# A decoder block on one core: experts' rows are added onto the residual rows in DRAM instead of being stored twice and summed at the end

## The reference, cut to what matters

```python
x = _layernorm(x + linear_attention(x))                       # 16 x 256 tokens of 256 features
x = _layernorm(x + cross_attention(x, ctx))
h = x + attention_over_the_batch_axis(layernorm1(x))          # hidden_after_attn, the residual rows
y = layernorm2(h)                                             # 4096 tokens
gate = softmax(y @ router.T); top_probs, top_idx = top_k(gate, 2)
expert_out[e] = gelu(y @ w1[e]) @ w2[e]                       # 8 experts, 256 -> 512 -> 256
x = _layernorm(h + sum_e weights[e] * expert_out[e])          # two experts for every token
```

## Time and profile before

| | |
|---|---|
| time, median of 3 runs | 800.7 us (794.5 to 801.46) |
| the profiled execution | 791.32 us, of which the span is 789.6 us |
| first scatter of the experts' loop | 477.25 us from the span's start |
| last scatter of the loop | 727.62 us |
| ending | from 730.07 us to the span's end |
| mean granted TensorE clock | 0.896 of full speed |

### The profile page before, as it was taken

One profiled execution on the slowest core, in us unless ns is written; L12 is line 12 of the kernel. 1 busy time (PEld: TensorE's weight loads), 2 busy tenths in 40 slices (PEclk: granted clock), 3 DMA queues, 4 the chain that ended last, 5 costly groups with the idle time before them and its releaser, 6 DMA issues.

```text
span 789.6 us, 19124 instructions
## 1 busy us (share of the span) xinstructions
PE 628.5 (80%) x5128; PEld 536.9 (68%) x5137; DVE 539.7 (68%) x1853; ACT 391.5 (50%) x923; POOL 321.0 (41%) x439
## 2 busy tenths in 40 slices
PE   4889999999961989999965139999999999997000
PEld 3678998898840667777755128888888888886000
DVE  1337878887855466888884836777777777775772
ACT  1335666656625556666534415555555555553233
POOL 0025777677643002566676722222222222222431
PEclk9989999999985899999976559999999999999555
DMA  6062444344311000111111422222222222221873
GB/s 196 0 177 71 143 133 113 106 138 123 97 28 27 1 2 2 42 56 57 56 56 68 154 91 70 72 80 68 79 68 79 69 80 68 80 68 47 279 245 114
DMA packets 48605, 69.19 MB, mean 88 GB/s; under 512 B 10577, under 2 KB 35281, under 8 KB 48561
## 3 DMA queue, kind: packets, MB, share of 16 engines
q1 hardware_dynamic: 40144, 46.30, 20.1%
q0 software_dynamic: 6480, 17.87, 6.1%
q10 hardware_dynamic: 1936, 4.46, 2.0%
HBM read 40.21 MB, written 24.19 MB: 82 GB/s over the span
## 4 chain that ended last, share of the span: by engine, by line
PE 42%; DVE 11%; DMA 5%; issue 3%; ACT 3%; POOL 3%; SPq 2%; DVEq 0%; POOLq 0%; ACTq 0%
PE half_bank L145 9%; PE half_bank L147 9%; PE half_bank L146 9%; PE half_bank L1856 5%; DMA out_dram<-all_w 3%; PE half_bank L1373 2%; PE half_bank L1837 2%; PE half_bank L1449 2%; POOL dispatched L949 2%; PE half_bank L1361 1%; DVE region_k_diag L1216 1%; ACT all_w L1615 1%; PE half_bank L1460 1%; DVE region_v_turned L1229 1%; DVE region_prob L1244 1%
## 5 line engine op out<-in xcount | busy, mean ns | idle before, releaser
L1675 POOL DMA_INDIRECT results<-all_w_qkv,ex_home x71 | 68.3, 961 | 200.6 <-DVE all_w_qkv L1800 170.5
L1707 ACT ACTIVATE region_hid_hi<-half_bank 128x256 fp32r<-128x256 f32 x142 | 46.9, 381 | 79.3 <-PE half_bank L1856 79.2
L949 POOL DMA_INDIRECT dispatched<-all_xh,all_slot_u x64 | 68.6, 1072 | 34.0 <-DVE all_slot_u L1318 17.4
L145 PE MATMUL half_bank<-region_w_hi,region_hid_hi 128*128 x284 | 81.2, 286 | 1.1 <-DVE region_hid_lo L1792 1.1
L146 PE MATMUL half_bank<-all_w,region_hid_hi 128*128 x284 | 79.7, 281 | 0.0
L147 PE MATMUL half_bank<-region_w_hi,region_hid_lo 128*128 x284 | 79.4, 280 | 0.0
L1694 ACT ACTIVATE all_xh<-half_bank,all_ln_b,all_ln_w 128x128 f32<-128x128 f32 x142 | 57.8, 467 | 21.0 <-PE half_bank L1837 21.0
L1800 DVE TENSOR_SCALAR all_w_qkv<-half_bank,ex_gate 128x256 f32<-128x256 f32 x71 | 34.3, 483 | 48.7 <-PE half_bank L147 48.7
L145 PE MATMUL half_bank<-region_w_hi,region_x_hi 128*128 x142 | 62.9, 443 | 0.7 <-DVE region_x_lo L1785 0.7
L1701 ACT ACTIVATE all_w_proj<-half_bank 128x512 f32<-128x512 f32 x71 | 42.5, 599 | 40.0 <-PE half_bank L147 40.0
L145 PEld LDWEIGHTS half_bank<-region_w_hi,region_hid_hi 128*128 128x128 f32 x284 | 53.3, 188 | 11.3 <-issue 7.8
(11 more groups left out here) (241 smaller groups left out, 1809.3 us busy)
## 6 DMA issues: line engine op xcount, KB each, us to landing
all_xh<-dispatched SPq DMA_DIRECT2D x71, 130.5 KB, 2.1
all_w<-in_moe_w_dram SPq DMA_DIRECT2D x32, 256.0 KB, 3.1
all_w<-results SPq DMA_DIRECT2D x12, 512.0 KB, 6.7
all_resid<-at_x SPq DMA_DIRECT2D x32, 128.5 KB
shared_x_t<-in_x_t_dram SPq DMA_DIRECT2D x16, 256.0 KB, 4.2
at_x_tok<-in_x_dram SPq DMA_DIRECT2D x16, 256.0 KB, 4.3
out_dram<-all_w ACTq DMA_DIRECT2D x6, 512.0 KB
dispatched<-all_tail SPq DMA_DIRECT2D x8, 261.0 KB, 3.3
```

Source lines behind the costliest of these rows:

```text
L145: nc.tensor.matmul(out, a_hi, b_hi, start=(start and i == 0), stop=False)
L949: nc.gpsimd.indirect_dma_start(out=dram["dispatched"], out_offset=bass.IndirectOffsetOnAxis(ap=keep["slot_u"][g % SENDS][:, u, k:k + 1], a ...
L1675: nc.gpsimd.indirect_dma_start(out=dram["results"], out_offset=bass.IndirectOffsetOnAxis(ap=home[par][:, 0:1], axis=0), in_=ym[par], in_of ...
L1707: nc.scalar.activation(hid_hi[par][:, cs, :], p_t[half], ACT.Copy).then_inc(s["hid_high"], 1)
```

## The change

The buffer `results` has one row for every token and the spare rows (4352 rows in place of 8448). SP stores the residual rows there (`store_base`), one group at a time: seven groups while the attention over the batch axis still runs, ahead of SP's other work there, and the last behind the first two loads of the experts' loop. GpSimd waits for all eight before its first scatter. Each scatter carries an addition, so a token's row collects the residual and both experts' rows. The place of a row is the token's number alone. The ending loads one sum per token. DVE's two additions go, and the freed space gives both the loads and the stores eight buffers.

```diff
-    DEPTH = 4
+    DEPTH = 8
...
-    y_rows = w1[:, :, :].rearrange("p k f -> p (k f)").rearrange("p (i k t d) -> p i k t d", i=DEPTH, k=2, d=D)
-    out_rows = w2[:, 0:2 * WIDEST, :].rearrange("p (i t) d -> p i t d", i=2)
+    y_rows = w1[:, :, :].rearrange("p k f -> p (k f)").rearrange("p (i t d) -> p i t d", i=DEPTH, d=D)
+    out_rows = w2[:, :, :].rearrange("p (i t) d -> p i t d", i=DEPTH)
...
         for j, (first, wide) in enumerate(TURNS):
             i = j % DEPTH
             wait(sp, out_ready, j - DEPTH + 1)
-            for k in range(2):
-                sp.dma_start(y_rows[:, i, k, 0:wide, :], dram["results_of"][k][:, first:first + wide, :])\
-                  .then_inc(y_in[i], 16)
+            sp.dma_start(y_rows[:, i, 0:wide, :], dram["sums"][:, first:first + wide, :]).then_inc(y_in[i], 16)
...
-        dve.wait_ge(keep["keep_done"], GROUPS * 2)
         for j, (first, wide) in enumerate(TURNS):
             i, par = j % DEPTH, j % 2
-            rows, more = y_rows[:, i, 0, 0:wide, :], y_rows[:, i, 1, 0:wide, :]
-            dve.wait_ge(y_in[i], (j // DEPTH + 1) * 32)
-            steps.chain(V.tensor_tensor(rows, rows, more, ALU.add))
-            steps.chain(V.tensor_tensor(rows, rows, keep["resid"][:, first:first + wide, 0:D], ALU.add))
+            dve.wait_ge(y_in[i], (j // DEPTH + 1) * 16)
             wait(dve, shift_ready, j - 1)
-            layer_norm_stats(steps, nc, rows, en_stats[par], en_mv[par], var_ready)
+            layer_norm_stats(steps, nc, y_rows[:, i, 0:wide, :], en_stats[par], en_mv[par], var_ready)
...
-            wait(act, out_stored[par], j // 2 * 16)
+            wait(act, out_stored[i], j // DEPTH * 16)
...
+        def store_base(g):
+            sp.wait_ge(keep["keep_done"], 2 * g + 2)
+            sp.dma_start(dram["sums"][:, g * NI:(g + 1) * NI, :], keep["resid"][:, g * NI:(g + 1) * NI, 0:D])\
+              .then_inc(base_out, 16)
+
+        for g in range(GROUPS - 1):
+            store_base(g)
         sp.wait_ge(s["tails_ready"], 1)
...
         load(0, 0)
         load(1, 1)
+        store_base(GROUPS - 1)
         with sp.Fori(0, (MOE_TILES - 3) // 2) as j:
...
             nc.gpsimd.indirect_dma_start(
                 out=dram["results"], out_offset=bass.IndirectOffsetOnAxis(ap=home[par][:, 0:1], axis=0),
-                in_=ym[par], in_offset=None).then_inc(ym_out[par], 16)
+                in_=ym[par], in_offset=None, compute_op=ALU.add).then_inc(ym_out[par], 16)
+        pool.wait_ge(base_out, GROUPS * 16)
         send(0, 0)
...
-            steps.chain(V.scalar_tensor_tensor(home_f[par][:, :], hit[:, 1:2], float(TOKENS), token[par][:, 0:1],
-                                               ALU.mult, ALU.add))
+            steps.chain(V.tensor_copy(home_f[par][:, :], token[par][:, 0:1]))
...
-        dram["results"] = scratch("results", [2 * TOKENS + 2 * P, D])
+        dram["results"] = scratch("results", [TOKENS + 2 * P, D])
```

More of the change, by code:

```diff
@@ L1022, in gpsimd_program @@
         nc.gpsimd.memset(tail[:, :, :], 0.0).then_inc(done, 1)
-        nc.gpsimd.iota(tail_no[:, :], [[P, 2]], base=2 * TOKENS, channel_multiplier=1,
+        nc.gpsimd.iota(tail_no[:, :], [[P, 2]], base=TOKENS, channel_multiplier=1,
                        allow_small_or_imprecise_dtypes=True).then_inc(done, 1)
@@ L1546, in experts @@
     ym_out = [m.sem(f"ym_out{i}") for i in range(2)]
+    base_out = m.sem("base_out")
     LAST = MOE_TILES - 1
@@ L1561, in experts @@
     y_in = [m.sem(f"y_in{i}") for i in range(DEPTH)]
-    out_stored = [m.sem(f"out_stored{i}") for i in range(2)]
+    out_stored = [m.sem(f"out_stored{i}") for i in range(DEPTH)]
     def end_sync(sp):
@@ L1611, in end_scalar @@
             i, par = j % DEPTH, j % 2
+            act.wait_ge(y_in[i], (j // DEPTH + 1) * 16)
             act.wait_ge(shift_ready, j + 1)
-            wait(act, out_stored[par], j // 2 * 16)
+            wait(act, out_stored[i], j // DEPTH * 16)
             for t in range(wide):
-                ins = nc.scalar.activation(out_rows[:, par, t, :], y_rows[:, i, 0, t, :], ACT.Identity,
+                ins = nc.scalar.activation(out_rows[:, i, t, :], y_rows[:, i, t, :], ACT.Identity,
                                            bias=en_shift[par][:, t:t + 1], scale=en_rstd[par][:, t:t + 1])
@@ L1618, in end_scalar @@
             act.wait_ge(out_ready, j + 1)
[L1619 to L1622, removed]
+            act.dma_start(dram["out_group"][:, :, first:first + wide, :], out_rows[:, i, 0:wide, :])\
+               .then_inc(out_stored[i], 16)
+        for i in range(DEPTH):
+            act.wait_ge(out_stored[i], (len(TURNS) + DEPTH - 1 - i) // DEPTH * 16)
     def moe_pipeline(first, step, end, repeat):
@@ L1973, in decoder_kernel @@
         dram["dispatched"] = scratch("dispatched", [E * SEGMENT, ROW])
-        dram["results"] = scratch("results", [2 * TOKENS + 2 * P, D])
-        dram["results_of"] = [dram["results"][k * TOKENS:(k + 1) * TOKENS, :].rearrange("(p i) d -> p i d", p=P)
-                              for k in range(2)]
+        dram["results"] = scratch("results", [TOKENS + 2 * P, D])
+        dram["sums"] = dram["results"][0:TOKENS, :].rearrange("(p i) d -> p i d", p=P)
         dram["out_group"] = dram["out"].rearrange("(t b i) d -> b t i d", t=B, b=P // B)
```

## The result

The changed kernel takes 857.61 us (856.08 to 862.22, 4 runs) against 800.3 us; the ratio is 1.0768, with a 95% interval from 1.0722 to 1.0814. It is slower by 57 us. The prediction said 817 and had the direction, and the range held the time, but the loss was three and a half times the 16.4 us that it forecast. The profiled execution took 856.08 us, its span is 854.3.

The account below looks back on a forecast made before the run. TensorE bounds the experts' loop, with GpSimd's scatter chain within 0.03 us of it; DMA engines hold the ending. Profiled 791.3 + 33.9 (loop) - 17.5 (ending) = 807.7, shifted to the median 817 us; range 778 to 880.

Parts of the forecast that it names:

- the break point L = 2.73: Experts' loop: scatter landing time L, in us, above which the chain of scatters, not TensorE, sets the period.
- The formula 71 L - 193.3 us: Experts' loop: how much later the last scatter lands for a landing of L us; 33.9 us at L = 3.2.
- The 0.85 us around a landing: Experts' loop: time the scatter chain's period adds to each landing, 3.25 - 2.4 us.
- The landing of an adding scatter: Experts' loop: L rises from 2.65 to 3.2 us; forecast case from 2.95 to 3.9, chance 0.50.
- a second stream of the same size adds 0.33: Scatter landing: the added read of 128 KB holds each DMA engine 0.33 us more, as the plain scatter's data does.
- The allowance of 0.22 for latency: Scatter landing: 0.22 us added for the part of the read that the first bytes must wait for.
- The side estimate of 3.18 us: Scatter landing by the Trainium skill's average HBM access: 2.65 + 0.33 + 0.2 = 3.18 us.
- the serial case: Rival, chance 0.18: the scatter's added read runs in series, L from 3.9 to 4.75 us, time 867 to 927 us.
- The count by engines: Ending: loads and stores on eight DMA engines fall from 51.7 to 39.3 us; with 2.7 us around them, 42 us.
- ACT's limit: Ending: ACT's work, ten issues, start and finish make 33.6 us, which would be a gain of 26 us.
- The hidden read: Rival, chance 0.25: the scatter's added read is hidden, L under 2.95 us, time 783 up to 799 us.
- The third: Rival, chance 0.07: smaller ending gain, 12.4 us or less, or last base store delays the first scatter; 825 us.

Follow-up runs that it names:

- the half rows: Changed kernel with scatters of only the first 128 of 256 columns of each row: 816.73 us with the addition, 765.44 us without.

## Why the prediction was right in kind and wrong in size

**What bounds the loop: right.** It named the chain of scatters as standing within 0.03 us of TensorE, and the break point L = 2.73. The formula 71 L - 193.3 us, with the measured L = 3.9, gives 83.6; the last landing measured from the first scatter came 80.7 later. The 0.85 us around a landing were 0.81 (4.71 - 3.9). Cutting the wait took the loss away and left the additions in.

**The landing of an adding scatter: the step that failed.** "I add 0.22 for the part of the read that the first bytes must wait for, so L = 3.2 us." It was 3.9, 0.7 more. By the prediction's own formula that is 71 x 0.7 = 50 us; the last landing came 80.7 us later and not 33.9, 46.8 more. Against the profiled execution (856.08 us for 807.7) the error is 48.4 us: these 46.8, 4.1 of a later first scatter, and 2.6 off for the ending. The medians lie only 40.6 us apart, since the 9.4 us that the forecast added to reach a median were 1.5 in the changed kernel; that part is luck. Two terms of L were off. The text held that of the 2.1 us of a serial load "the rest ... is issue and completion, which a scatter pays once anyway", and that the issue stays at about 0.96; it grew by 0.58, and the issue lies inside the landing. And "a second stream of the same size adds 0.33": it added 0.61 on each engine, since the packets of an addition hold an engine 2.8 times as long as those of a plain scatter (0.94 against 0.33 us), not twice. The allowance of 0.22 for latency happened to cover most of the missing 0.28, so that after the issue the forecast of 0.55 stood against 0.62. That is luck too, since the half rows show that the time on the engines and the landing do not grow together. What was missed is the issue: 0.58 of the 0.7. The side estimate of 3.18 us left it out in the same way. The range held the time because the serial case was priced.

**The ending: 42 us forecast, 39.4 measured,** a gain of 20.1 against 17.5. The count by engines (39.3 us of loads and stores on eight engines) came near, but not for the reason given. ACT's own chain, 2.82 us a turn, was the last wait from 826.7 us on, over half of the ending, and the store buffers, for which the forecast had no term of their own, were half of the gain. ACT's limit had been put at 33.6 us; among other things the last issue, at 846.6, stood 7.7 us before the end and not 4.6. DVE's additions were taken to be covered; the chain of the kernel with eight store buffers runs through them.

**Base stores, DVE, first scatter: right,** nothing that shows. The kernel without the addition has them all and is 21.6 us faster than before. The eighth base store of the changed kernel was issued at 467.3 us and not at 463; no view gives its landing, and the chain that ended last comes to the first scatter through TensorE and DVE's tile.

**What the profile was to show:** the period and TensorE's idle time as told, though the latter 16% and not 12%. "The releaser of nearly all of them the DMA" was wrong as a reading: the view names DVE, as shown above, and only the chain shows the landing.

**The rivals.** The hidden read (0.25) is out, its bound of 2.95 far from 3.9. The serial one began at 3.9, where the landing lies; but the runs do not bear out a read in series, which would have added 2.1 us behind the issue: half of the growth is in the issue, and 0.62 comes after it. The third, a smaller gain in the ending or a base store that holds the first scatter, did not come.

## What to carry to other kernels

Before an operation is put on an engine that looks idle, look for a chain through it: issue, landing, wait, issue. Its period, and not the engine's busy time, is to be held against the bound of the loop, and once the chain sets the pace every tenth of a microsecond in it counts once per turn. When a chain is long because two DMAs might touch the same rows, ask which pairs can: here a count from a table turned a change of +7.7% into one of -2.2%. In this ending eight store buffers were worth 3.2 us by themselves and 9.8 beside the rest of the change, so an edit that shows nothing alone can be worth trying again once the limit has moved.

## What the runs showed of the hardware that was not expected

In the experts' loop an indirect scatter of 128 rows costs GpSimd 0.96 us to issue and 1.54 with an addition, whatever the width of the rows; with 64 rows 1.41. After the issue an adding scatter of 128 KB needs 2.36 us to land against 1.74, and each of its rows is a packet of its own (9 packets an engine with the last, 5 with 64 rows, against 3 for the plain one of full width: 3216 packets in 67 scatters on 16 engines). With the wait kept only at experts the queue's share rises more than the number of scatters does: 32.4% of the engines at 56 scatters in 200 us, against 20.2% at 43, which is 18.5 against 15.0 engine-us for each, with the loop undisturbed; whether that is because two can be in flight is not shown. Stores in 4 KB rows kept up with ACT's 186 GB/s at about half of the engines' time; in 8 KB rows, split by 16 partitions, 201 GB/s took 84% of it.
